# Zero products of 128x32 among the 32x32 block products of a delta-rule and mixture-of-experts kernel

## The reference, cut to what matters

```python
def step(S, inp):
    q_t, k_t, v_t, g_t, b_t = inp
    S = S * jnp.exp(g_t)[..., None, None]
    pred = jnp.einsum('bhk,bhkv->bhv', k_t, S)
    delta = (v_t - pred) * b_t[..., None]
    S = S + k_t[..., None] * delta[..., None, :]
    o = jnp.einsum('bhk,bhkv->bhv', q_t, S)
    return (S, o)
```

## Time and profile before

| what | value |
|---|---|
| runs | 1155.61, 1166.93, 1169.36 us |
| the profiled execution's own time | 1162.42 us |
| its span, first to last instruction | 1160.6 us |
| PE busy | 971.9 us (84%) |
| DVE, ACT, POOL busy | 696.9, 489.6, 641.9 us |
| mean granted TensorE clock | 0.849 |

### The profile page before, as it was taken

The page is one execution under the profiler, slowest core; times in us unless marked ns, Lnnn a source line. Parts: engine busy times, 40 slices in busy tenths (PEclk is TensorE's granted clock), DMA queues, the critical chain, the costliest instruction groups (busy, mean ns, idle before and its releaser), DMA issues.

```text
span 1160.6 us, 32029 instructions
## 1 busy us (share of the span) xinstructions
PE 971.9 (84%) x12359; PEld 826.5 (71%) x12359; DVE 696.9 (60%) x1703; ACT 489.6 (42%) x932; POOL 641.9 (55%) x783
## 2 busy tenths in 40 slices
PE   4876899989898988999789889974886989999970
PEld 3765788778787878878778877873784657777760
DVE  6378957667765865776585476668443444333338
ACT  5524445345453543545364354531522234444430
POOL 3041348858875885787688578645031115555550
PEclk8686888879778887988997697797778989999995
DMA  6737036649348654933956540111147234444429
GB/s 234 228 77 189 1 69 177 169 115 279 97 127 216 175 170 131 276 103 107 261 129 174 153 98 29 34 39 37 69 202 285 92 96 132 129 131 129 128 47 359
DMA packets 181826, 165.33 MB, mean 142 GB/s; under 512 B 75427, under 2 KB 174124, under 8 KB 180784
## 3 DMA queue, kind: packets, MB, share of 16 engines
q10 hardware_dynamic: 72208, 73.96, 22.5%
q1 hardware_dynamic: 101840, 72.47, 21.3%
q0 software_dynamic: 7632, 16.87, 4.5%
HBM read 65.76 MB, written 101.55 MB: 144 GB/s over the span
## 4 chain that ended last, share of the span: by engine, by line
PE 43%; POOL 15%; DVE 14%; issue 10%; DMA 4%; another core or an unknown queue 2%; ACT 2%; SPq 1%; POOLq 0%; DVEq 0%; ACTq 0%
PE ps L1531 5%; POOL arena L785 5%; POOL arena L782 5%; PE ps L1615 4%; DVE arena L1119 4%; PE ps L1396 3%; POOL nrm L748 3%; PE ps L1548 3%; PE ps L1450 3%; PE ps L1460 3%; PE ps L1606 2%; PE ps L1429 2%; PE ps L1440 2%; PE ps L1406 2%
## 5 line engine op out<-in xcount | busy, mean ns | idle before, releaser
L1119 DVE SCALAR_TENSOR_TENSOR arena<-ps,cw,arena 128x256 f32<-128x256 f32 x384 | 155.4, 475 | 42.8 <-ACT arena L907 42.5
L1396 PE MATMUL ps<-work,arena 128*128 128x259 f32 x512 | 159.7, 469 | 15.4 <-DVE arena L1119 9.2
L1396 PEld LDWEIGHTS ps<-work,arena 128*128 128x128 f32 x512 | 116.5, 236 | 41.7 <-DVE arena L1119 10.4
L837 POOL DMA_INDIRECT picked<-work x95 | 93.4, 984 | 94.8 <-issue 48.7
L826 POOL DMA_INDIRECT slotted<-hr,slots x64 | 63.7, 996 | 102.6 <-DVE slots L1270 86.4
L785 POOL TENSOR_TENSOR arena<-arena 128x31 f32<-128x31 f32 (+15 forms) x186 | 111.1, 597 | 14.6
L1303 DVE TENSOR_TENSOR work<-work,ps 128x128 f32<-128x128 f32 (+1 forms) x111 | 34.0, 307 | 138.7 <-ACT work L1018 113.3
L1615 PE MATMUL ps<-arena,work 128*128 x380 | 101.3, 389 | 6.1 <-issue 5.0
L782 POOL TENSOR_TENSOR arena<-arena 128x31 f32<-128x31 f32 (+15 forms) x186 | 96.0, 516 | 12.4
L907 ACT ACTIVATE arena<-ps,cw 128x256 f32<-128x256 f32 x128 | 58.1, 470 | 76.6 <-PE ps L1396 60.7
L807 POOL TENSOR_TENSOR work<-work,ec 128x512 f32<-128x512 f32 x32 | 33.7, 1053 | 101.7 <-PE ps L1489 82.5
(11 more groups left out here) (224 smaller groups left out, 2262.6 us busy)
## 6 DMA issues: line engine op xcount, KB each, us to landing
slotted<-blank ACTq DMA_DIRECT2D x17, 4128.0 KB, 18.9
arena<-in_w SPq DMA_DIRECT2D x2, 6528.0 KB, 27.3
arena<-tab SPq DMA_DIRECT2D x96, 128.0 KB, 4.0
work<-slotted SPq DMA_DIRECT2D x95, 129.0 KB
arena<-picked SPq DMA_DIRECT2D x16, 512.0 KB, 9.5
work<-tab SPq DMA_DIRECT2D x32, 128.0 KB, 3.7
arena<-in_w_qkv SPq DMA_DIRECT2D x1, 2048.0 KB, 7.5
xin<-in_x SPq DMA_DIRECT2D x16, 128.0 KB, 4.8
```

Source lines behind the costliest of these rows:

```text
L837: g.indirect_dma_start(out=picked, out_offset=bass.IndirectOffsetOnAxis(ap=to, axis=0), in_=yrow[:, j % SLOTS, :], in_offset=None, bounds_ ...
L1119: v.scalar_tensor_tensor(out=acc_, in0=bank_of("proj", p, s_, i)[:, k:k + W2], scalar=cw[:, u, k:k + 1], in1=acc_, op0=ALU.mult, op1=ALU.a ...
L1396: ins = mm(to[:, 0:WX], wqkv[:, k, m:m + P], xt2[:, p % 3, k, :], start=k == 0, stop=k == KD - 1)
```

## The change

One product is added in the loop of pm and one in that of tm, at every fourth turn of a loop of 32 turns with two products each. So there are 8 more products in a stage, one ahead of every 8 block products: 128x32 zeros as the stationary operand, the identity with its 128 columns as the moving one. It contracts over all 128 partitions and writes zeros over 32 output partitions of the stage's first bank, 128 columns: partitions 0 to 31 in pm and 32 to 63 in tm, which the block products of the stage don't write. Two helper functions are added that nothing calls.

```diff
+            def add_zeros(to, times):
+                for _ in range(times):
+                    mm(to[:, 0:P], blank[:, 0:P], ident, start=False, stop=False)
+
+            def put_zeros(to, times):
+                for _ in range(times):
+                    mm(to[:, 0:P], blank[:, 0:P], ident, start=True, stop=True)
+
...
                     pe.wait_ge(S["xt_turned"], 2 * p + 2)
                     for m in range(2 * NV):
+                        if m % 4 == 0:
+                            mm(to[0][0:H, 0:P], blank[:, 0:H], ident, start=True, stop=True)
                         for e in range(2):
...
                     pe.wait_ge(S["pe_out"], 2 * p + 2)
                     for m in range(2 * NV):
+                        if m % 4 == 0:
+                            mm(to[0][H:C, 0:P], blank[:, 0:H], ident, start=True, stop=True)
                         for e in range(2):
```

## The result

The changed kernel takes 1247.43 us in the median of four runs (1244.29 to 1255.40), the kernel before 1164.17 us in the four runs beside it: a ratio of 1.073, with a 95% interval from 1.065 to 1.082. The forecast was 1227 us, +65; it came out at +83 by the medians and +85 by the ratio. The direction and the prices of a zeros product hold. The sum is too small, by the clock above all, and the top of the range, 1248, lies between the median and the 1249.5 us that 1164.17 times the ratio gives. A ratio leaves out single slow executions, over 1.5% above the fastest of the same kernel, and a median has them in.

What follows compares the result with a forecast made beforehand. PE, nearly full and partly at 1.2 GHz, was taken to bound the kernel, with both merge stages on the chain. Seven pairs at +8.2 (57) and 7.5 for the last, about +65 on 1162.4, gave 1227 us; range 1176 to 1248.

Steps and rivals of the forecast that it cites:

- One zeros product: In pm and tm: columns plus two changes of shape, 0.45 us at full clock, 0.7 at half; stage +3.4 or +5.6.
- The third case: In pm and tm: zeros cost almost nothing and hold the clock; 1141 us, or 1155 at L1471's price; chance 0.12.
- What the clock can give back: From kb to rt and in kk: a clock held at 1.00 returns at most 3.1 us a pair.
- What the clock does in the changed kernel: In pm and tm: half clock for half of each stage, +4.5 each, 0.8 back behind; +8.2 us a pair.
- The second case: From pm to kk: the clock holds at 1.00, +3.7 us a pair; 1195 us; chance 0.18.
- The last pair: pm stands between dense stages with nothing like kb between the two: +3.4 and about +4.1, 7.5 us.
- One for one along the chain: Between pm and kk: a microsecond more is a microsecond more for the pair, in eight pairs, with no slack expected.
- the fourth case: In pm and tm: zeros do nothing for the clock, half clock from early on, 11.2 us a pair; 1248 us; chance 0.10.

Runs made afterwards that it cites:

- one-column run: Against the kernel before: the zeros products in both stages move 1 column instead of 128; 1211.85 us, ratio 1.040.
- same-shape run: Against the kernel before: zeros products in both stages in the blocks' own shape, contracting over 32 partitions, 128 columns; 1173.58 us, ratio 1.007.
- zeros in pm's wait: Against the kernel before: five 128x128 zeros products into a free PSUM bank ahead of pm's wait, first seven pairs; 1144.16 us, ratio 0.992.
- doubled blocks: Against the kernel before: each block product of both stages stands twice, no zeros; 1225.75 us, ratio 1.053.
- two at four places: Against the kernel before: eight zeros products a stage, in four groups of two ahead of every 16 block products; 1204.56 us, ratio 1.045.
- the gate product in pm's wait: Against the kernel before: fourth gate product of the first seven pairs moved between kt and pm, output to UR, eviction later; 1140.41 us, ratio 0.988.

## Why the prediction was right and wrong

**One zeros product: right.** Its parts were each within a few hundredths: a group 0.89 to 0.93 us at full clock (0.90), 1.14 to 1.16 at half (1.17). The one-column run isolates the changes of shape, which no row of before showed for 128*32: 0.25 to 0.29 us for a pair of them at full clock and 0.31 to 0.34 at half. Taken were 0.16 + 0.10 and 0.16 + 0.15, each less the 0.03 of the one step that the 0.16 stands in for: 0.23 and 0.28.

The Trainium skill, "TensorEngine Tiling (Array Packing)", Tiling Modes, has a drain at each change of mode, and the one-column run agrees. The Trainium skill, "TensorE: Matmul & The Clock Gate", Part 3, has products in different tiles of the array overlap, and the same-shape run agrees, +0.3 and +0.03 us a stage. Both hold, each in its place: in these runs products overlap within one shape and not across a change of it.

**The third case, zeros that cost almost nothing:** falls by the one-column run. Its break-even, 0.19 us for a zeros product, is already passed by the drains.

**What the clock can give back: right as a price.** kb to rt takes 3.09 us where the clock held, 2.3 less than 5.41 (2.4 forecast). The whole section takes 13.2 us where the clock holds from end to end (zeros in pm's wait, pair 3), 2.8 less than the 16.0 before; 3.1 was the most forecast.

**What the clock does in the changed kernel: the step that failed.** I took the clock at half for half of each stage, +4.5 each, and 0.8 back behind them. pm grew by 5.0 in the mean of the seven pairs, at a clock of 0.55 to 0.65, tm by 4.6. Of kb to rt I took 0.6 back and got 0.2, and kk to u gave nothing (+0.1, forecast -0.2). That makes 9.5 a pair instead of 8.2, or 9 us in seven: 0.5 of the 1.3 is pm, 0.1 tm, and 0.7 what didn't come back. The step that failed is the choice of the middle between a held and a lost clock: the zeros in singles don't hold it. By the granted clock and the length of pm, it stayed at 2.4 GHz for 0.9 to 2.6 us from pm's start, and for 1.2 to 2.8 us before the change (an estimate from the stretches of the seven pairs), so it was lost as early as before, and more of the zeros then ran at half clock. tm was about as forecast. The second case, a held clock, came about with two zeros products in a row in six of eight pairs, and there the extra columns cost what the clock saved.

**The last pair:** forecast 7.5, measured 10.0. I had held that there was nothing like kb between its stages. There are the sixteen L1548 (L1560 after), part of which ran at half clock once pm had lost it (0.60 in the mean): 6.01 us instead of 3.65. That is 2.4 of the 2.5 us that were missing.

**One for one along the chain: right in the section, incomplete behind it.** The doubled blocks give 62 us for 60. The changed kernel has 77 in its section and 83 to 85 by the medians and the ratio. So the miss of 18 us by the medians is 9 in the seven sections, 2.5 in the last, and some 6 outside, for which the sum had no term. Where these lie is not settled. The seven stretches from u to the next pm hold the same products in both kernels; they are 14.3 us longer in the profiled execution of the changed kernel (586.9 against 572.6), PE being busy 7.9 us longer, at a mean clock of 0.87 instead of 0.88, and idle 6.4 us longer. In kernels whose edit leaves these stretches alone as well, they come out from 8 us shorter (two at four places) to 14 us longer (one column), so chance is not excluded. In the two profiled executions, PE's waits for su (L1188) behind it grew by 4 us, as they did by 3 with the doubled blocks, and other stretches of a pair gain and lose a few us with where the clock falls. PE's waits by what ended them (us in total, times, longest) in the changed kernel:

```profile
PE ps L1491 <- DVE work L1188: 18.5, 11, 2.7
```

and in the kernel before, where that product is L1479:

```profile
PE ps L1479 <- DVE work L1188: 14.4, 10, 2.8
```

I had left no room for that: the fourth case, at 1248, should have stood below the top of the range and not at it. The measured time is that of the fourth case, though its reason falls, and it is reached by other terms: not both stages at half clock throughout, but pm mostly, tm in part, nothing given back, and what lies outside.

## What to carry to other kernels

A product put in to keep TensorE's clock, of another shape than its neighbours, is paid in full where the engine's list is on the chain: its columns, and twice a drain. In its neighbours' own shape it was nearly free here, but did nothing for the clock in pm. Put such work where PE idles, in one block, or move real dense work there: the gate product in pm's wait gave 14 us, and zeros in the same wait 10 (the two are not clearly apart), where full-height zeros in the stages or right ahead of their blocks cost 12 to 86. And before filling a wait, look up which semaphore ends it: the releaser's line is in the row.

## What the runs showed of the hardware that I had not expected

- A 32*32 product of 128 columns among 32*32 products of 32 columns costs next to nothing where it stands (with eight of them tm takes 3.80 against 3.77 us, pm 4.05 to 4.31 against 3.8), though it streams four times the columns.
- Eight zeros products with 128*32 of the array ahead of pm held 0.93 to 1.00 through it; eight spread singly through pm, the same products, left it at 0.55 to 0.65 in seven pairs; two at each of the eight places held 1.00 in six of eight pairs. All three had PE busy throughout.
- PE stands still inside one run of products with nothing in the profile to wait for. In the changed kernel, in a u product of pair 1, with the DMA engines busy:

```profile
287.38 0.71 PE L1511 MATMUL ps<-work 64*64 64x64 f32 x18
...
291.41 0.68 PE L1511 MATMUL ps<-work 64*64 64x64 f32 x13 [3.31 <-issue]
```

Such waits between 60 and 930 us sum to 19 us in the kernel before and 21 in the changed one, and they fall in different places in each kernel. They go with the transfers of queue 8, which the profile's table of DMA queues calls `instruction` and which has about 100 packets of 0.02 MB in a kernel. In the thirteen profiled executions of this case there are 107 such waits of over 1 us between 60 and 930 us; 73 of them ended 1.2 to 1.7 us after one of these packets had, where chance would give about 5%. So late instructions are the likely cause of most; no run varied it, and what makes them late is not shown.
